# Query tiles 1 and 0 joined into one step of a hand-ordered attention pipeline

## What is computed

```python
a1 = _attn(q, k1, v1, causal=True)     # keys and values from a latent
a2 = _attn(q, ks, vs, causal=False)    # 32 selected tokens
a3 = _attn(q, kw, vw, causal=True)     # keys and values from the input
out = g[:, 0] * a1 + g[:, 1] * a2 + g[:, 2] * a3
return out.transpose(0, 2, 1, 3).reshape(B, T, N_HEAD * V_HEAD) @ w_proj
```

## Time and profile before

| | |
|---|---|
| time, median of 3 runs | 2321.69 us (2316.57 to 2322.24) |
| profiled execution | 2312.3 us, span 2310.5 us |
| busy, share of the span | TensorE 83%, VectorE 59%, ScalarE 50%, GpSimd 28% |
| mean granted TensorE clock | 0.90 |
| layer 0 and preparation | up to about 378 us |
| attention stage | about 378 to 2262 us |

### The profile page before, as it was taken

How to read it: one execution, slowest core, us unless ns; L and a number is a source line. 1 busy time by engine, 2 the same in 40 slices (tenths; PEclk the granted TensorE clock), 3 DMA queues, 4 the chain that set the end, 5 groups by cost and what they waited for, 6 DMA issues and landing times.

```text
span 2310.5 us, 40290 instructions
## 1 busy us (share of the span) xinstructions
PE 1911.7 (83%) x10620; PEld 1069.9 (46%) x10620; DVE 1367.5 (59%) x4228; ACT 1163.8 (50%) x3476; POOL 645.1 (28%) x659
## 2 busy tenths in 40 slices
PE   3433357999899998999899989999899899989985
PEld 2221224555445544555455545555455455545542
DVE  5999833656555555555555555555565655565563
ACT  1112213656556565556465655565565556556651
POOL 0323233323323332323232322323232323332200
PEclk7556556999999998989998999899998999899998
DMA  3000002111101110111111111111111111111101
GB/s 137 0 0 0 0 14 53 44 41 36 51 19 40 35 50 23 36 32 40 36 34 36 42 43 33 33 46 42 34 33 45 42 34 33 35 52 31 35 1 37
DMA packets 71349, 81.44 MB, mean 35 GB/s; under 512 B 29521, under 2 KB 37842, under 8 KB 70994
## 3 DMA queue, kind: packets, MB, share of 16 engines
q1 hardware_dynamic: 71122, 78.74, 13.2%
HBM read 7.90 MB, written 2.10 MB: 4 GB/s over the span
## 4 chain that ended last, share of the span: by engine, by line
PE 69%; DVE 17%; issue 8%; ACT 3%; DVEq 1%; POOL 1%; SPq 1%; DMA 0%; ACTq 0%; POOLq 0%
PE bank L1652 21%; PE bank L1672 14%; PE bank L1612 9%; DVE arena L1349 4%; PE bank L1522 4%; PE bank L1523 4%; DVE arena L1341 3%; PE bank L1623 2%; PE bank L1564 2%; PE bank L1545 2%; PE bank L1518 1%; PE bank L1577 1%; PE bank L1560 1%; DVE arena L1106 1%; PE bank L1585 1%
## 5 line engine op out<-in xcount | busy, mean ns | idle before, releaser
L1341 DVE CUSTOM_DVE_ANT_0 arena<-bank,W 128x512 f32<-128x512 f32 (+3 forms) x1024 | 502.0, 490 | 711.4 <-PE bank L1652 573.4
L1652 PE MATMUL bank<-arena 96*128 96x512 f32 (+6 forms) x2048 | 785.6, 466 | 30.8 <-issue 18.3
L903 ACT ACTIVATE arena<-arena 128x512 f32<-128x512 f32 (+3 forms) x1024 | 572.8, 559 | 442.5 <-DVE arena L1341 439.2
L1672 PE MATMUL bank<-W,arena 128*128 128x128 f32 x2560 | 487.1, 288 | 97.1 <-DVE arena L1349 92.0
L1672 PEld LDWEIGHTS bank<-W,arena 128*128 128x128 f32 x2560 | 306.2, 142 | 464.3 <-DVE arena L1349 226.0
L1652 PEld LDWEIGHTS bank<-arena 96*128 96x128 f32 x2048 | 341.1, 199 | 174.6 <-issue 149.7
L1349 DVE COPY arena<-bank 128x512 f32<-128x512 f32 (+2 forms) x768 | 356.2, 464 | 2.0 <-issue 1.5
L685 POOL TENSOR_TENSOR arena<-arena,one 128x512 f32<-128x512 f32 x64 | 66.7, 1042 | 950.6 <-DVE arena L1311 939.7
L1612 PE MATMUL bank<-arena 128*32 128x256 f32 (+1 forms) x3072 | 227.6, 369 | 8.3 <-DVE arena L1349 7.7
L903 ACT ACTIVATION_READ_ACCUMULATOR arena<-arena 128x1 f32 x1024 | 194.8, 190 | 0.0
L886 ACT ACTIVATE arena<-bank 128x384 f32<-128x384 f32 x256 | 125.6, 491 | 116.2 <-PE bank L1672 116.0
(11 more groups left out here) (260 smaller groups left out, 2259.3 us busy)
## 6 DMA issues: line engine op xcount, KB each, us to landing
arena<-arena SPq DMA_DIRECT2D x896, 64.0 KB, 2.0
arena<-arena SPq DMA_DIRECT2D x64, 128.0 KB, 2.4
W<-wide SPq DMA_DIRECT2D x1, 3730.0 KB, 13.3
X<-x SPq DMA_DIRECT2D x8, 256.0 KB, 5.5
out<-arena SPq DMA_DIRECT2D x8, 256.0 KB, 2.2
arena<-arena SPq DMA_DIRECT2D x96, 16.0 KB, 1.9
LW<-lat SPq DMA_DIRECT2D x1, 768.5 KB, 14.3
arena<-mods SPq DMA_DIRECT2D x1, 768.0 KB, 4.5
```

What stands on the lines that cost most here:

```text
L903: A(Pb[:, s % 4, 0:n], Pb[:, s % 4, 0:n], ACT.Exp, bias=nmax[:, s:s + 1], scale=-1.0, accum_out=lsum[:, c:c + 1]).then_inc(s_p, 1)
L1341: v.tensor_tensor_reduce(Pb[:, s % 4, 0:n], bank[turn.score_bank(s)][:, lo:lo + n], w("mask", T - n), -1.0, 3e38, ALU.add, ALU.min, nmax[: ...
L1652: MM(bank[turn.score_bank(s)][:, 0:lo + n], query(t), Kb[a][0:QD, g % 2, h, skip:skip + lo + n], start=True, stop=True).then_inc(s_qk, 1)
L1672: last = pe.transpose(bank[3 + k % 2][:, c * P:(c + 1) * P], Pb[:, k % 4, c * P:(c + 1) * P], ident)
```

## The change

Tiles 1 and 0 of a head become one step. A row has 12 steps (8 tall, 4 joined), a group 24, a turn 96. Both tiles' scores lie side by side in one bank (`laid` gives the columns: 384 in row 1, 480 with the selected ones in row 0). A joined step has two or three score matmuls, two masked maxima, the copies of selected scores, two exponentials with a row sum each, three transposes (blocks in the order 0, 2, 1) and one copy of 384 columns by VectorE into `PT[1]`. Tile 2's blocks are still moved by ScalarE, tile 3's by VectorE. `D_LAG` goes from 3 to 2, and all step numbers (tasks, values, row and cell work) are set anew for 24 steps. The matrix work, the masks and the sums stay.

```diff
-HALVES = ((3, 2), (1, 0))
+STEPS = ((3,), (2,)), ((1, 0),)
@@
-    return [(q, h, a, t) for q in range(groups) for a in range(2) for half in HALVES for h in range(HG) for t in half]
+    return [(q, h, a, tiles) for q in range(groups) for a in range(2) for half in STEPS for h in range(HG) for tiles in half]
+def laid(a, tiles):
+
+    at, out = 0, []
+    for t in reversed(tiles):
+        lo = scores_at(a, t)
+        out.append((t, (t + 1) * P, lo, at))
+        at += lo + (t + 1) * P + (lo if t == 0 else 0)
+    return out[::-1]
@@
-T_LAG, D_LAG = 2, 3
-PV_TALL, PV_LOW = 11, 19
-INVERT, SPREAD, MOVE, NORM, ADD = 16, 19, 21, 23, 24
-MOVER = {3: "dve", 2: "act", 1: "dve", 0: "dve"}
+T_LAG, D_LAG = 2, 2
+PV_TALL, PV_LOW = 10, 14
+INVERT, SPREAD, MOVE, NORM, ADD = 12, 14, 15, 16, 17
+MOVER = {3: "dve", 2: "act", 1: "dve"}
@@ group_tasks
-    steps, proj, extra = {"op": 12, "p2T": 22, "o2": 24}, (0, 2, 4, 7, 8, 13, 15, 17, 19), []
+    steps, proj, extra = {"op": 8, "p2T": 18, "o2": 20}, (0, 2, 4, 6, 7, 9, 11, 13, 15), []
     if g == 0:
-        steps, proj = {"op": 11, "p2T": 23, "o2": 25}, (1, 2, 4, 7, 8, 13, 15, 27, 30)
-        extra = [] if first else [(17, "z4T"), (20, "gf"), (21, "gi"), (24, "gc")]
+        steps, proj = {"op": 7, "p2T": 18, "o2": 20}, (0, 1, 3, 5, 6, 9, 10, 21, 22)
+        extra = [] if first else [(12, "z4T"), (14, "gf"), (15, "gi"), (19, "gc")]
     if g == 2 and not last:
-        steps, proj = {"op": 11, "p2T": 22, "o2": 24}, (1, 2, 4, 7, 8, 13, 14, 16, 17)
-        extra = [(19, "cqkv"), (23, "kr"), (27, "sel"), (28, "ks"), (30, "nqT")]
+        proj = (0, 1, 3, 5, 6, 9, 10, 11, 12)
+        extra = [(15, "cqkv"), (17, "kr"), (19, "sel"), (21, "ks"), (22, "nqT")]
     if g == 3 and not last:
-        steps, proj = {"op": 11, "p2T": 22, "o2": 24}, (2, 3, 6, 7, 9, 13, 15, 17, 19)
-        extra = [(27, "vs")]
+        proj = (1, 2, 4, 6, 7, 10, 11, 13, 15)
+        extra = [(22, "vs")]
@@ ScalarE
-                        A(Pb[:, s % 4, 0:n], Pb[:, s % 4, 0:n], ACT.Exp, bias=nmax[:, s:s + 1], scale=-1.0,
-                          accum_out=lsum[:, c:c + 1]).then_inc(s_p, 1)
+                        for t, n, lo, at in laid(a, tiles):
+                            c = turn.col(s, t)
+                            here = Pb[:, s % 4, at_p:at_p + n]
+                            done = A(here, here, ACT.Exp, bias=nmax[:, c:c + 1], scale=-1.0, accum_out=lsum[:, c:c + 1])
+                            at_p += n
+                        done.then_inc(s_p, 1)
@@ VectorE
-                        v.tensor_tensor_reduce(Pb[:, s % 4, 0:n], bank[turn.score_bank(s)][:, lo:lo + n], w("mask", T - n), -1.0, 3e38,
-                                               ALU.add, ALU.min, nmax[:, s:s + 1]).then_inc(s_max, 1)
+                        for t, n, lo, at in laid(a, tiles):
+                            c = turn.col(s, t)
+                            last = v.tensor_tensor_reduce(Pb[:, s % 4, at_p:at_p + n],
+                                                          bank[turn.score_bank(s)][:, at + lo:at + lo + n],
+                                                          w("mask", T - n), -1.0, 3e38, ALU.add, ALU.min, nmax[:, c:c + 1])
+                            at_p += n
+                        last.then_inc(s_max, 1)
@@ VectorE, group 0
-                        if at == 13:
+                        if at == 9:
                             v.wait_ge(s_gd, turn.read("op", q - 1))
...
-                        if at == 16:
+                        if at == 11:
                             normed_out(turn.b)
@@ TensorE
-                        for c in range(t + 1):
-                            last = pe.transpose(bank[3 + k % 2][:, c * P:(c + 1) * P], Pb[:, k % 4, c * P:(c + 1) * P], ident)
+                        order = (0, 2, 1) if tiles[0] == 1 else range(tiles[0] + 1)
+                        for n, c in enumerate(order):
+                            last = pe.transpose(bank[3 + k % 2][:, n * P:(n + 1) * P], Pb[:, k % 4, c * P:(c + 1) * P], ident)
```

More of the change, by code:

```diff
@@ L130, in __init__ @@
         self.n1 = len(self.units) + (ADD - RU + 1 if self.last else 0)
-        self.c0 = (NG - 1) * GU if self.first else 0
+        self.c0 = (NG - 1) * GR * NT * HG if self.first else 0
     def filled(self, name, k=0):
@@ L469, in turned @@
         def turned(turn, k):
-            _, h, _, t = turn.units[k]
-            low, at = int(t < 2), (t % 2 == 0) * P
-            return PT[low][:, h, at:].rearrange("p (c x) -> p c x", x=P)[:, 0:2 * t + 1:2]
+            _, h, _, tiles = turn.units[k]
+            if tiles[0] == 1:
+                return PT[1][:, h]
+            return PT[0][:, h, (tiles[0] == 2) * P:].rearrange("p (c x) -> p c x", x=P)[:, 0:2 * tiles[0] + 1:2]
         def turned_bank(turn, k):
-            t = turn.units[k][3]
-            return bank[3 + k % 2][:, 0:(t + 1) * P].rearrange("p (c x) -> p c x", x=P)
+            tiles = turn.units[k][3]
+            blocks = bank[3 + k % 2][:, 0:sum(t + 1 for t in tiles) * P]
+            return blocks if tiles[0] == 1 else blocks.rearrange("p (c x) -> p c x", x=P)
         block = ctx.enter_context(nc.Block())
@@ L1308, in row_inverted @@
                         v.wait_ge(s_ix, r0 + (r - 1))
-                    step(v.reciprocal(inv[:, r % 2], lsum[:, turn.c0 + r * RU:turn.c0 + (r + 1) * RU] if r >= 0 else lsum[:, NG * GU - RU:]))
+                    step(v.reciprocal(inv[:, r % 2], lsum[:, turn.row_cols(r)]))
                     step.settle()
@@ L1333, in attend @@
                     if s < n_units:
[L1334 to L1335 removed]
+                        _, _, a, tiles = turn.units[s]
                         v.wait_ge(s_qk, u0 + (s + 1))
@@ L1627, in attend @@
                     if s < n_units:
-                        q, h, a, t = turn.units[s]
-                        g, n = turn.g(q), (t + 1) * P
+                        q, h, a, tiles = turn.units[s]
+                        g = turn.g(q)
                         if s % GU == 0:
@@ L1642, in attend @@
                             before = s - 2 if s < 2 else s - 3
-                            _, _, a3, t3 = turn.units[before]
-                            pe.wait_ge(s_p if scores_at(a3, t3) else s_max, u0 + (before + 1))
-                        lo = scores_at(a, t)
-                        skip = 0 if lo or a else KEEP
+                            _, _, a3, tiles3 = turn.units[before]
+                            pe.wait_ge(s_p if scores_at(a3, tiles3[0]) else s_max, u0 + (before + 1))
+                        B_ = bank[turn.score_bank(s)]
                         query = lambda t: Qb[0:QD, g % 2, h, t * P:(t + 1) * P]
-                        if lo and t == 0:
-                            MM(bank[turn.score_bank(s)][:, lo + n:lo + n + KEEP], query(NT - 1), Kb[0][0:QD, g % 2, h, 0:KEEP],
-                               start=True, stop=True)
-                        MM(bank[turn.score_bank(s)][:, 0:lo + n], query(t), Kb[a][0:QD, g % 2, h, skip:skip + lo + n],
-                           start=True, stop=True).then_inc(s_qk, 1)
+                        for t, n, lo, at in laid(a, tiles):
+                            skip = 0 if lo or a else KEEP
+                            last = MM(B_[:, at:at + lo + n], query(t), Kb[a][0:QD, g % 2, h, skip:skip + lo + n],
+                                      start=True, stop=True)
+                            if lo and t == 0:
+                                at += lo + n
+                                last = MM(B_[:, at:at + KEEP], query(NT - 1), Kb[0][0:QD, g % 2, h, 0:KEEP],
+                                          start=True, stop=True)
+                        last.then_inc(s_qk, 1)
                     for low, at, parts in ((0, PV_TALL, 4), (1, PV_LOW, 2)):
```

90 lines of the change are left out of this document (47 added, 43 removed).

## The result

The changed kernel takes 2130.1 us (median of 4 runs, 2122.7 to 2132.3) against 2322.0 before (2316.6 to 2323.0): ratio 0.917, 95% interval 0.915 to 0.920, faster by 192 us. The forecast was 2188 us, with 2110 to 2295 as the range and a "faster way" at 2120.

What follows compares the result with a forecast made beforehand. The prediction took TensorE waiting on VectorE's late turned-block copies as the bound; -24 + 4 + 1 + 2 = -17 us a turn, 7.9 times, 134 us off the profiled 2312.3, gave a 2188 us median, range 2110 to 2295.

Steps and rivals of the forecast that it cites:

- faster way: Rival: copy stall nearer 36 us a turn, little takes its place, and the clock recovers; put at 2120 us, chance 0.20.
- The bound: Attention loop: TensorE, VectorE, TensorE over the turned-block copies sets the end, 24 us stall a turn; TensorE content most of the rest.
- Part 1: Copy one step earlier (D_LAG 3 to 2): removes 24 us a turn, bounds 12 and 36; VectorE's waits cost 0.
- Part 2: Tiles 1 and 0 joined: fewer steps and copies, 0.15 us less VectorE copying 8 times a group, off the bound: 0.
- Part 3: Longer scores-to-transposes chains in joined steps, covered by value sets or shared-bank matmuls: cost 0, at most 16 us a turn.
- Part 4: Shared bank's tasks in 24 steps: neighbouring tasks in joined steps wait for ScalarE reads, +4 us a turn, bounds 0 and 6.
- Part 5: Moved row work: GpSimd rotations 0, norm ahead of z4T +1 us a turn, VectorE's extra operations in steps 12 to 17 +2.
- likeliest case: The main forecast of 2188 us, with 2150 to 2260 us given chance 0.60.
- The signs: Copy waits under 3 and 10 us, turn about 222, VectorE and ScalarE busy within 5, joined steps 1.6 to 2.6 us.
- signs of being wrong: Weight loads waiting over 30 us a turn for exponentials or shared-bank reads, joined steps above 2.69 us, or longer half-clock stretches.
- TensorE is the bound already: Rival: TensorE's 92% busy is real, stall only 12 us a turn; 2282 to 2322 us, chance 0.10 together with no effect.
- The slower one: Rival: ScalarE's queue closes the joined steps' chain without cover, 3.0 us a step; 2345 us as a middle, chance 0.10.

Runs made afterwards that it cites:

- lag2_old: The kernel before with only D_LAG 3 to 2, so VectorE moves turned blocks two steps after the scores; 2175.7 us, ratio 0.940.
- double_old: The kernel before, with VectorE copying each turned block row of tile 3 twice, first into an unread spare tile; 2415.0 us, ratio 1.041.
- tlag3: The changed kernel with transposes and copies three steps behind the scores instead of two, value sets and row work one step later; 2149.7 us, ratio 0.926.
- lag2_pv: The changed kernel, D_LAG still 2, with only the value sets and their row work one step later; 2103.8 us, ratio 0.908.
- tasks2: The changed kernel with x2k not right behind x1k, p2T and o2 one step later in groups 1 and 3, vw and vl in group 3; 2107.6 us.
- tasks: The changed kernel with x2k not behind x1k, p2T and o2 later in groups 0, 1, 3; part of selected attention computed from other data; 2093.4 us.
- dve_all: The changed kernel with tile 2's turned blocks moved by VectorE as well, so ScalarE moves none; 2163.9 us, ratio 0.933.

## Why the prediction was right, and where it wasn't

*The bound.* Right: the loop TensorE, VectorE, TensorE over the late copies set the end. lag2_old shows it, and double_old shows that time added to the copy is seen. But the stall was nearer to 17 us than to the 24 in the middle of the bracket. The 24.2 us of the table's copy column agree with 24 only because they hold the time that value sets carry in every kernel: behind a set the transposes start 0.57 or 0.36 us after its start before the change too, and 16.1 us stand ahead of transposes that follow scores.

*Part 1, the copy a step earlier.* Right in kind, too large in size: lag2_old gives 17.4 us a turn where "removed" stands at 24, and in the table's copy column 24.2 fell to 7.4 in the changed kernel, so 16.8 went. The rest was never a wait for a copy. "Cost 0" for VectorE's waits held. That the forecast's total of 17 a turn equals lag2_old's 17.4 is chance: its copy term was 7 too large, and the 7 that it added for parts 4 and 5 has no counterpart in lag2_old.

*Part 2, joining.* Its term was 0, and that is the term that failed. With the early copy held the same, joining takes 2175.7 to 2130.1, 46 us or 6.3 us a turn (lag2_old against after; 40 us by the two profiled executions, 52 by the ratios, since lag2_old's four runs spread over 16 us). This is the joining with all its new step lists, which no run separates. By my working 1.7 of these 6.3 us are streaming, through the clock, and 4.6 idle time: 3.4 less ahead of scores for their bank, which is asked for 25% less often, 1.2 less for copies, 0.9 less for ScalarE's reads, 1.0 less for VectorE's (z4T's wait of 2.8 us is gone, p2T's of 2.4 has come, both by moved steps), and 2.1 more in the column of the exponential. I had priced the engines' work in the joined steps, found none on the path, and left out the places where TensorE waits for a bank: 96 steps have fewer than 128. That this is the reason for the 3.4 us fits, but is argued and not tested. The copy of 384 columns, bounded by 0.42 and 0.69 and taken as 0.55, took 0.557 us:

```profile
L1375 DVE COPY arena<-bank 128x384 f32<-128x384 f32 x32 | 17.8, 557 | 4.3 <-PE bank L1702 3.8
```

*Part 3, the longer chain.* Right: cost 0. tlag3 loosened the chain and gained nothing.

*Part 4, tasks in neighbouring steps.* The size was near by luck (4 forecast, 3.4 measured ahead of L1549 by the starts of the matmuls, 0.6 at the same place before), the place wrong. The joined steps, where I put it, show no such wait. It sits in tall steps, ahead of x2k behind x1k, and the new lists aren't its only cause: lag2_old, with the old lists, already has 1.1 us a turn there and 1.4 ahead of x2q behind x1q, which the changed kernel hasn't. A queue that I had costed at 0 in part 5 has a share: in two of the four places the rotations on GpSimd hold x1k's read, 0.9 us a turn together.

*Part 5, moved row work.* +1 for z4T was wrong in sign: of the 2.4 us a turn by the starts of the matmuls before, nothing above 0.3 is left. +2 for VectorE's operations was near: p2T's wait for L1320 is 2.4 us in the turn (0.8 a turn for the same operation before, by the starts of the matmuls). What the prediction missed altogether is the step of the value sets and of the row work behind them, worth 25 us (lag2_pv): no term of the sum spoke of it.

*The sum.* -17 us a turn was forecast, -23.7 measured (192 us over the whole run, 8.1 times that). The difference of 6.7 us by terms: the copies gave 7.2 less (16.8 instead of 24); all other idle time fell by 2.8 where +7 was added for it, 9.8 more; and streaming fell by 4.1 through the clock, which the sum hadn't. The half-clock time fell from 21.0 to 7.3 us a turn; the faster rival had this mechanism, with up to 7 us a turn. So the likeliest case had the right main cause and was too small, and the time came out near the faster way (2120) with two of its reasons out of three: not a larger stall, but nothing in its place, and the clock.

*The signs.* The copy waits fell to none and 2.8 us a turn (under 3 and 10 were named) and the busy times stayed within 5 us; only the turn was shorter than 222 us, and none of the signs of being wrong came.

*The rivals.* "TensorE is the bound already" fell with the first run. The slower one, ScalarE's queue in joined steps, would have needed them above 2.69 us; by medians over the seven turns the 32 joined steps of a turn take 74.2 us, 2.3 each with their tasks and sets (single ones mostly between 1.4 and 3.1, so the 1.6 to 2.6 that the prediction named holds for the mean alone), and tlag3 shows no chain there. But the tall steps became longer, 129.4 to 141.1 us a turn for 64 steps, with the same tasks in fewer steps; the low halves fell from 111.4 to 74.2.

*What stays open.* Whether lag2_pv and the task steps of tasks2 add up to some 2080 us wasn't tried; both take away the wait ahead of x2k, so they may not add. What joining alone brings, apart from its step lists, isn't separated. Nor is it settled that tasks2 spends more time at half clock than tasks: its profile is of the slowest of its four runs (2114.4 us at a mean granted clock of 0.906; the fastest took 2098.5 at 0.914), and that of tasks had 0.913.

## What to carry to other kernels

In a pipeline ordered by hand, write down for each buffer the loop that frees it, with every instruction that stands ahead in each queue, and compare it with the steps it spans: one step's lag of a copy behind its producer was worth 6% here, three times what joining the steps, with their new lists, brought on top. When steps are renumbered, the distance from each producer to its consumer (value sets, shared-bank reads, a third engine's buffer) has to be checked one by one; one step of the value sets and their row work cost 25 us in the changed kernel and 128 us with late copies. A wait that is named by the last semaphore is only shown to be one when loosening that semaphore removes it.

## What the runs showed of the hardware

Behind a set of value matmuls that use 32 columns of the array each, full-array transposes start 0.15 us later than the streaming accounts for (0.57 against 0.43 us after the set's start, 0.36 against 0.21), at the full clock in every kernel, and whatever semaphore stands between.

The granted clock followed small changes of the order. Two of the changed kernel's half-clock stretches (columns as in the earlier trace rows):

```profile
957.00:963.80 6.80, 6.80 (x34) 4.37 (x34) 3.43 (x16) 1.82 (x6) 0.00 (x0) 0.50 0.09 15
1073.00:1076.40 3.40, 3.40 (x7) 1.33 (x5) 1.73 (x6) 1.41 (x3) 1.04 (x1) 0.50 0.01 2
```

At 0.50 (0.51 in the earlier trace rows, cut a little wider) the clock is at the lower of its two levels, 1.2 GHz. TensorE's records fill both stretches. By the starts of the matmuls, its longest idle time in the 7 us ahead of them was 0.7 us at 957.0 and 2.7 us at 1073.0. None in the loop lasts longer than 6.9 us, where the one of the earlier trace rows lasted 14.0. Between kernels with the same matmuls a turn held from 3.9 us (dve_all) to 26.3 us (double_old) at half clock, and its streaming time went from 177.0 to 184.6 us with it. The Trainium skill ("TensorE: Matmul & The Clock Gate", Part 1) says that idleness throttles the clock; the order of the kernels by idle time agrees only roughly, since dve_all, which is slower than the changed kernel, has less time at half clock than it.
